# Eight-expert transformer tower on one core: the middle stage's steps in another order, and h1 carried inside the routed rows

## Chip, cores and metric

The kernel is one program on 1 core of one Trainium2 chip. The metric is the device time of one execution in microseconds. Before the change it is 1646.1 us (median of 3 runs, 1643.71 to 1647.52).

## What is computed

x holds 16 images of 256x256. The reference runs five parts on them; every LayerNorm here is over the last axis.

```python
h = tok(x)                                   # three Haar levels, gated, and put together again
h = _layernorm(h + attention(h))             # 16 heads; this is h1 in the kernel
h = _layernorm(h + ffn0(h))                  # h2: top 2 of 8 experts, 256 -> 512 -> 256
h = _layernorm(h + L1_attn(h))               # h3, see below
h = _layernorm(h + ffn1(h))                  # top 1 of 8 experts, 256 -> 1024 -> 256

# ffn0
gates, expert_idx = jax.lax.top_k(probs, K)  # K = 2
out = jnp.einsum('ne,nec->nc', weights, expert_out)

# L1_attn
attn_out = quantum_circuit(xh)               # cumprod(cos(v)) over groups of 16
x1 = layer_norm(x + attn_out, gamma1, beta1)
q = quantum_circuit(x1[..., :nq])            # nq = 16
h = jnp.einsum('btq,fq->btf', q, w1) + b1
ffn_out = jnp.einsum('btf,cf->btc', jax.nn.relu(h), w2) + b2
return layer_norm(x1 + ffn_out, gamma2, beta2)
```

## The kernel before

The program has four stages, one behind the other, with a barrier (the semaphores quiet0, quiet1, quiet2) between them.

**Attention** makes h1 image by image (16 images of 256 tokens, two tiles of 128 partitions each). Its step `nrm` writes h1 to a tile of rows of 264 words: 256 of h1, two expert numbers, two gates, two target rows, and two words that are zero. `rows` scatters each row twice to `rows0_d`, one copy per chosen expert. `store` (L387 to L389, SyncE) writes h1 itself to `h1_d` in HBM, and `nrm` waits for it two images later (L1008).

**First experts** (`experts`) takes 71 tiles of 128 routed rows. Per tile GpSimd gathers the rows (L1123), TensorE transposes, multiplies, transposes and multiplies (L1155, L1164, L1186, L1176), and VectorE adds the first bias (L1256). `owner` (L1237 to L1249) then finds for each row which of its two choices this expert is, its gate and its target row. `g2` adds the second bias (L1263) and multiplies by the gate (L1266). GpSimd sends the result to `y0_d` (L1128), whose first 4096 rows are the first choices and whose next 4096 are the second.

**Middle** (`middle`) takes 16 images again. The order on all engines comes from one list, STEPS. Each engine walks through it once per turn and runs those steps that it has a function for, with an image number that the second word gives as an offset to the turn:

```python
STEPS = [("load", "n2"), ("A1", "n"), ("root0", "n"), ("h2", "n"), ("SC", "m"), ("root1", "m"), ("RTa", "n"), ("x1", "m"),
         ("T", "p"), ("XQ", "m"), ("qsin", "m"), ("D", "p"), ("rk", "p"), ("RTb", "n"), ("sin", "n"), ("prep", "n"),
         ("SQa", "m"), ("qc", "m"), ("x1g", "m"), ("R2", "f"), ("root2", "f"), ("SQb", "m"), ("F1", "m"), ("R", "p"), ("scatter", "p"),
         ("B2", "f"), ("A0", "n1"), ("root3", "f"), ("h2b", "n"), ("F2", "m"), ("h3", "f")]
AHEAD = {"n2": 2, "n1": 1, "n": 0, "m": -1, "f": -2, "p": -3}
```

So in a full turn four images are under way. The steps, by what they do:

- A0 (GpSimd, L1415): h1 + first choice. A1 (VectorE, L1689): that + second choice, then its mean and variance (variances 0: L1671, L1674, and the negated mean, L1681).
- root0 to root3 (GpSimd, L1419 to L1424): 1/sqrt of a variance and the offset. h2 (ScalarE, L1557): the normalized h2; its second half (L1570, L1572) counts the whole turns in the cosine's argument. h2b (GpSimd, L1438): h2 + beta2.
- RTa, RTb (VectorE, L1695, L1702): the argument less whole turns. sin (ScalarE, L1594 to L1597): the cosines. SC (VectorE, L1709, L1711): the running products by a scan, + h2, variances 1. x1 (ScalarE, L1557): the normalized x1. x1g (GpSimd, L1431): x1 * gamma1.
- XQ, qsin, SQa, qc, SQb (L1720 to L1727, L1606 to L1609, L1734, L1616 and L1617, L1739): the same circuit on 16 columns of x1.
- F1 (TensorE L1483 and L1490, ScalarE L1623 and L1628): transposes, first product and Relu. F2 (TensorE L1499 to L1506): second product. R2, B2 (VectorE): variances 2, then z2 and r3 (L1753, L1762) and variances 3. h3 (ScalarE): the normalized h3.
- T (TensorE L1516 and L1524, ScalarE L1634): h3 transposed and the logits. D (VectorE L1773 to L1783): the choice. rk (TensorE), R (VectorE L1788 to L1794): ranks. scatter (GpSimd L1444, L1447): two indirect DMAs of h3's rows.
- prep (all engines, for image 0 only): the weights transposed; on SyncE it prefetches the next stage's weights.

Numbers of images count from 0; "turn" below means one pass through STEPS, and a full turn is one in which all four images exist (13 of them, with A1 of images 3 to 15).

**Last experts** takes 39 tiles of h3 and is not touched.

## Time and profile before

| | us |
|---|---|
| median of 3 runs | 1646.1 |
| profiled execution | 1646.75 |
| its span, first to last instruction | 1644.9 |
| TensorE busy | 1301.9 (79%) |
| VectorE busy | 930.9 (57%) |
| GpSimd busy | 733.7 (45%) |
| ScalarE busy | 526.1 (32%) |

The page writes PE for TensorE, PEld for its weight loads, DVE for VectorE, ACT for ScalarE, POOL for GpSimd and SP for SyncE (SPq is its queue, where DMAs are issued). Busy time is an average over the four stages, which have different limits; so the windows and the timelines of single stages matter more than these shares. In a timeline a row gives the start, the duration, the engine, the line, the operation with output and input, and in brackets how long the engine sat idle before and what ended that. Attention ends at about 613 us, first experts at 917, middle at 1305.

### The profile page before, as it was taken

To read this page: it belongs to the slowest core of one execution; us is meant where nothing else is said; L and a number is where in the kernel's file an instruction comes from. 1 tells how busy PE (TensorE), PEld (TensorE's weight loads), DVE (VectorE), ACT (ScalarE), POOL (GpSimd) and SP (SyncE) were. 2 spreads that over 40 slices of the span, in tenths; PEclk is the share of its full clock that TensorE was granted. 3 is DMA by queue.
4 is the path that set the end of the run, shared out by engine and by line. 5 is a ranking of instruction groups with operands and counts; after the bars stand their busy time and mean duration, and the time that the engine had idled before them with its cause. 6 is when DMAs were issued, how large, how long until landed. Compare 5 with 4: busy or idle time off the path is not lost.

```text
span 1644.9 us, 23467 instructions
## 1 busy us (share of the span) xinstructions
PE 1301.9 (79%) x6856; PEld 913.8 (56%) x6856; DVE 930.9 (57%) x2664; ACT 526.1 (32%) x998; POOL 733.7 (45%) x926
## 2 busy tenths in 40 slices
...
DMA packets 97448, 134.69 MB, mean 82 GB/s; under 512 B 18208, under 2 KB 80302, under 8 KB 96304
## 3 DMA queue, kind: packets, MB, share of 16 engines
...
q10 hardware_dynamic: 3376, 1.22, 0.4%
q8 instruction: 61, 1.00, 0.3%
...
## 4 chain that ended last, share of the span: by engine, by line
PE 57%; DVE 16%; POOL 9%; issue 6%; ACT 5%; DMA 4%; SPq 1%; another core or an unknown queue 1%; ACTq 0%; DVEq 0%; POOLq 0%
PE ebank L1942 8%; PE ebank L1953 8%; PE ebank L1164 8%; PE ebank L1176 7%; PE mbank L1506 4%; PE bank L597 3%; DVE top_a_a L967 2%; PE ebank L1963 2%; PE ebank L1186 2%; PE bank L679 2%; PE av_bank L653 2%; POOL fine_a L454 1%; PE s_bank L620 1%; DVE product_a L852 1%; DMA prob_a<-in_L_attn_Wo 1%
## 5 line engine op out<-in xcount | busy, mean ns | idle before, releaser
L967 DVE TENSOR_REDUCE top_a_a<-s_bank 128x4 f32<-128x1024 f32 x128 | 156.5, 1223 | 122.6 <-PE s_bank L620 113.2
L796 ACT ACTIVATE prob_a<-s_bank 128x1024 f32<-128x1024 f32 x128 | 130.4, 1019 | 80.7 <-PE s_bank L641 76.9
L1942 PE MATMUL ebank<-w,exT 128*128 x312 | 143.0, 602 | 0.7 <-ACT exT L1988 0.7
L1506 PE MATMUL mbank<-w2T_m,fhT_m 128*128 128x256 f32 x512 | 143.0, 443 | 0.0
L1953 PE MATMUL ebank<-w,ehT 128*128 x624 | 141.2, 379 | 0.9 <-ACT ehT L1996 0.9
L1164 PE MATMUL ebank<-w,exT 128*128 x284 | 135.4, 600 | 0.6 <-ACT exT L1211 0.6
L1176 PE MATMUL ebank<-w,ehT 128*128 x568 | 134.4, 380 | 0.8 <-ACT ehT L1217 0.8
L1506 PEld LDWEIGHTS mbank<-w2T_m,fhT_m 128*128 128x128 f32 x512 | 119.0, 232 | 23.1
L1123 POOL DMA_INDIRECT ex<-rows_d,tile_row x71 | 72.8, 1025 | 119.6 <-DVE sent_to L1249 103.6
L1953 PEld LDWEIGHTS ebank<-w,ehT 128*128 128x128 f32 x624 | 115.6, 190 | 15.7 <-issue 1.6
L531 POOL DMA_INDIRECT rows_d<-h_a,row_i_a x64 | 63.7, 995 | 128.8 <-DVE row_i_a L1053 113.8
L1176 PEld LDWEIGHTS ebank<-w,ehT 128*128 128x128 f32 x568 | 102.5, 190 | 12.5 <-issue 1.5
L1256 DVE TENSOR_TENSOR eh<-ebank,b 128x512 f32<-128x512 f32 x71 | 49.1, 692 | 104.9 <-PE ebank L1164 103.5
L2027 DVE TENSOR_TENSOR eh<-ebank,b 128x512 f32<-128x512 f32 x78 | 54.0, 692 | 84.9 <-PE ebank L1942 84.9
L620 PE MATMUL s_bank<-ks_a,qs_a 48*128 48x256 f32 x512 | 67.6, 344 | 31.7 <-DVE top_a_a L967 19.2
L1128 POOL DMA_INDIRECT y_d<-ey,sent_to x71 | 72.2, 1017 | 42.4 <-issue 27.9
L1942 PEld LDWEIGHTS ebank<-w,exT 128*128 128x128 f32 x312 | 57.2, 193 | 58.7 <-issue 58.7
L1996 ACT ACTIVATE ehT<-ebank 128x512 f32<-128x512 f32 x78 | 42.3, 595 | 138.7 <-PE ebank L1963 138.7
L1419 POOL TENSOR_SCALAR rstd_m_m<-moments_m_m 128x2 f32<-128x2 f32 x64 | 34.2, 535 | 115.8 <-DVE moments_m_m L1674 88.9
L1217 ACT ACTIVATE ehT<-ebank 128x512 f32<-128x512 f32 x71 | 42.4, 597 | 131.6 <-PE ebank L1186 129.7
L620 PEld LDWEIGHTS s_bank<-ks_a,qs_a 48*128 48x128 f32 x512 | 42.0, 202 | 72.4 <-issue 48.2
L641 PE MATMUL s_bank<-qs_a,ks_a 50*128 50x256 f32 x512 | 66.5, 340 | 17.2 <-DMA qs_a<-shiftT_a 13.9
...
## 6 DMA issues: line engine op xcount, KB each, us to landing
...
```

Of the source, the lines that this page charges most:

```text
L531: pool.indirect_dma_start(out=rows0_d, out_offset=bass.IndirectOffsetOnAxis(ap=row_i[i % 2][:, t, k:k + 1], axis=0), in_=h1[i % 2][:, t, : ...
L620: last = nc.tensor.matmul(s1_bank[:, g, t * SEQ:(t + 1) * SEQ], qs[i % RING][rows, j, t * P:(t + 1) * P], ks[i % RING][rows, j, :], start= ...
L641: last = nc.tensor.matmul(s2_bank[:, g, t * SEQ:(t + 1) * SEQ], ks[i % RING][rows, j, t * P:(t + 1) * P], qs[i % RING][rows, j, :], start= ...
L796: nc.scalar.activation(prob[:, j % 4].rearrange("p g t s -> p (g t s)"), s2_bank[:].rearrange("p g s -> p (g s)"), ACT.Exp, scale=HD ** -0 ...
L967: nc.vector.tensor_reduce(top[:, j].rearrange("p g t -> p (g t)"), s1_bank[:].rearrange("p g (t s) -> p (g t) s", t=TPI), axis=AX, op=ALU. ...
L1123: pool.indirect_dma_start(out=x[j % XR][:].bitcast(I32), out_offset=None, in_=rows_d, bounds_check=E * SLOTS - 1, oob_is_err=False, in_off ...
L1128: pool.indirect_dma_start(out=y_d, out_offset=bass.IndirectOffsetOnAxis(ap=sent_to[j % YR][:], axis=0), in_=y[j % YR][:], in_offset=None, ...
L1164: last = nc.tensor.matmul(bank[1 + j % 2][:], xT[j % 2][:, ch, :], w[:, bass.ds(e, 1), width * ch:width * (ch + 1)].rearrange("p a f -> p ...
L1176: last = nc.tensor.matmul(bank[4 + j % 2][:, 0:D], hT[j % 2][:, f, :], w[:, bass.ds(e, 1), at:at + D].rearrange("p a d -> p (a d)"), start ...
L1506: last = nc.tensor.matmul(b[:, t * D:(t + 1) * D], hT[:, f, t * P:(t + 1) * P], w2T[:, f, :], start=False, stop=f == FC - 1)
L1942: last = nc.tensor.matmul(bank[1 + n % 2][:], xT[j % 2][:, ch, :], w[:, bass.ds(e, 1), at:at + 512].rearrange("p a f -> p (a f)"), start=c ...
L1953: last = nc.tensor.matmul(bank[4 + j % 2][:, 0:D], hT[j % 2][:, f, :], w[:, bass.ds(e, 1), at:at + D].rearrange("p a d -> p (a d)"), start ...
```

## The change

Two things change.

1. **h1 travels with the rows.** The two spare words of each row now hold 1.0 for the first choice and 0.0 for the second. `owner` picks that word together with the gate and the target row, and writes h1 times it (h1 or nothing) to the result tile y. `g2` adds the second bias into a tile of its own, and then computes gate * result + y in one operation. So `y0_d`'s first half holds h1 + first choice. `h1_d`, its stores in attention, its loads in middle, the semaphores for both and step A0 are gone; A1 adds the two halves.
2. **STEPS in another order**, with h2's second half as a step of its own (tn), and F1's transposes as a step of their own (qT). The offsets stay.

```diff
--- attention
-                 ("p2_6", "t"), ("av_2", "t"), ("p1_6", "n"), ("tprd_4", "n2"), ("lg", "p"), ("store", "p"),
+                 ("p2_6", "t"), ("av_2", "t"), ("p1_6", "n"), ("tprd_4", "n2"), ("lg", "p"),
...
-            def store(i):
-                sp.wait_ge(q["h1_ok"], i + 1)
-                sp.dma_start(h1_v[i], h1[i % 2][:, :, 0:D]).then_inc(h1_out[i % 2], 16)
...
-                c.run(nc.gpsimd.memset(h1[u][:, :, D:ROW0], 0.0))
+                c.run(nc.gpsimd.memset(h1[u][:, :, D + 6:D + 7], 1.0))
+                c.run(nc.gpsimd.memset(h1[u][:, :, D + 7:D + 8], 0.0))
...
-                    dve.wait_ge(h1_out[i % 2], 16 * (i // 2))
--- experts
                 c.link(nc.vector.scalar_tensor_tensor(
-                    out=chosen[:], in0=tail[:, D:D + 2].unsqueeze(1).to_broadcast([P, 2, 2]), scalar=tile_sum[:, j:j + 1],
-                    in1=tail[:, D + 2:D + 6].rearrange("p (a k) -> p a k", k=2), op0=ALU.is_equal, op1=ALU.mult))
+                    out=chosen[:], in0=tail[:, D:D + 2].unsqueeze(1).to_broadcast([P, 3, 2]), scalar=tile_sum[:, j:j + 1],
+                    in1=tail[:, D + 2:D + 8].rearrange("p (a k) -> p a k", k=2), op0=ALU.is_equal, op1=ALU.mult))
                 c.link(nc.vector.tensor_reduce(own[u][:], chosen[:], axis=AX, op=ALU.add))
-                nc.vector.tensor_tensor(sent_to[u][:], own[u][:, 1:2], outside[:, j:j + 1], ALU.max).then_inc(own_ok, 1)
+                c.run(nc.vector.tensor_tensor(sent_to[u][:], own[u][:, 1:2], outside[:, j:j + 1], ALU.max))
+                nc.vector.tensor_scalar(y[u][:], tail[:, 0:D], own[u][:, 2:3], None, ALU.mult).then_inc(own_ok, 1)
...
-                nc.vector.tensor_tensor(y[u][:], bank[4 + j % 2][:, 0:D], b[:, bass.ds(e, 1), width:width + D].rearrange("p a f -> p (a f)"),
+                if j >= 1:
+                    dve.wait_ge(y_ok, j)
+                nc.vector.tensor_tensor(result[:], bank[4 + j % 2][:, 0:D], b[:, bass.ds(e, 1), width:width + D].rearrange("p a f -> p (a f)"),
                                         ALU.add).then_inc(biased, 1)
                 dve.wait_ge(biased, j + 1)
-                nc.vector.tensor_scalar(y[u][:], y[u][:], own[u][:, 0:1], None, ALU.mult).then_inc(y_ok, 1)
+                dve.wait_ge(own_ok, j + 1)
+                nc.vector.scalar_tensor_tensor(out=y[u][:], in0=result[:], scalar=own[u][:, 0:1], in1=y[u][:], op0=ALU.mult, op1=ALU.add).then_inc(y_ok, 1)
--- middle
-        STEPS = [("load", "n2"), ("A1", "n"), ("root0", "n"), ("h2", "n"), ("SC", "m"), ("root1", "m"), ("RTa", "n"), ("x1", "m"),
...
+        STEPS = [("load", "n2"), ("A1", "n"), ("root0", "n"), ("SC", "m"), ("h2", "n"), ("root1", "m"), ("x1", "m"), ("h2b", "n"), ("tn", "n"),
+                 ("XQ", "m"), ("qsin", "m"), ("T", "p"), ("RTa", "n"), ("RTb", "n"), ("prep", "n"), ("SQa", "m"), ("R2", "f"), ("x1g", "m"),
+                 ("qc", "m"), ("SQb", "m"), ("sin", "n"), ("root2", "f"), ("D", "p"), ("qT", "m"), ("rk", "p"), ("B2", "f"), ("root3", "f"),
+                 ("R", "p"), ("F1", "m"), ("h3", "f"), ("scatter", "p"), ("F2", "m")]
...
             constants()
-            for i in range(RING):
-                load_h(i)
             sp.wait_ge(s["quiet1"], 4)
-            load_y(0)
-            load_y(1)
+            load(0)
+            load(1)
             more_constants()
-            load_y(2)
+            load(2)
...
-            def A0(i):
-                u = i % RING
-                pool.wait_ge(h_in[u], 32 * (i // RING + 1))
-                nc.gpsimd.tensor_tensor(hin[u][:], hin[u][:], ya[u][:], ALU.add).then_inc(q["part_ok"], 1)
...
-                dve.wait_ge(q["part_ok"], i + 1)
-                dve.wait_ge(y_in[u], 16 * (i // RING + 1))
+                dve.wait_ge(y_in[u], 32 * (i // RING + 1))
...
-                nc.vector.tensor_tensor(flat(sum_), flat(hin[u]), flat(yb[u]), ALU.add).then_inc(q["sum_ok"], 1)
+                nc.vector.tensor_tensor(flat(sum_), flat(ya[u]), flat(yb[u]), ALU.add).then_inc(q["sum_ok"], 1)
```

How the new list moves instructions, at three places.

GpSimd in middle, from one image's scatter to the next image's root0, before. In these rows moments and off belong to root3, then root0, and h_0, h_1 are tiles of h3 (from token) or h2 (for h2b):

```order
L1444 COPY h_0_m<-token_m 128x2x4
L1447 DMA rows_d<-h_0_m,row_i_m 33792x260 x2
L1415 TENSOR_TENSOR hin_m<-hin_m,ya_m 128x512
L1419 TENSOR_SCALAR rstd_m_m<-moments_m_m 128x2
L1423 TENSOR_TENSOR rstd_m_m<-rstd_m_m,minus_half 128x2
L1424 TENSOR_TENSOR off_m_m<-minus_m_m,rstd_m_m 128x2
L1438 TENSOR_TENSOR h2b_m<-h_1_m,a_be_m 128x512
L1419 TENSOR_SCALAR rstd_m_m<-moments_m_m 128x2
L1423 TENSOR_TENSOR rstd_m_m<-rstd_m_m,minus_half 128x2
L1424 TENSOR_TENSOR off_m_m<-minus_m_m,rstd_m_m 128x2
```

and with the change, from root3 on, where root3, scatter, root0, root1 and h2b follow one another:

```order
L1403 TENSOR_SCALAR rstd_m_m<-moments_m_m 128x2
L1407 TENSOR_TENSOR rstd_m_m<-rstd_m_m,minus_half 128x2
L1408 TENSOR_TENSOR off_m_m<-minus_m_m,rstd_m_m 128x2
L1428 COPY h_0_m<-token_m 128x2x4
L1431 DMA rows_d<-h_0_m,row_i_m 33792x260 x2
L1403 TENSOR_SCALAR rstd_m_m<-moments_m_m 128x2
L1407 TENSOR_TENSOR rstd_m_m<-rstd_m_m,minus_half 128x2
L1408 TENSOR_TENSOR off_m_m<-minus_m_m,rstd_m_m 128x2
L1403 TENSOR_SCALAR rstd_m_m<-moments_m_m 128x2
L1407 TENSOR_TENSOR rstd_m_m<-rstd_m_m,minus_half 128x2
L1408 TENSOR_TENSOR off_m_m<-minus_m_m,rstd_m_m 128x2
L1422 TENSOR_TENSOR h2b_m<-h_0_m,a_be_m 128x512
```

A0 (L1415) is gone, the scatter stands behind root3 and directly ahead of root0, and h2b behind root1.

ScalarE in middle, from h3 to x1, before:

```order
L1557 ACTIVATE h_1_m<-r_m,off_m_m,rstd_m_m 128x256 x2
L1557 ACTIVATE h_0_m<-sum__m,off_m_m,rstd_m_m 128x256 x2
L1570 ACTIVATE turnsn_m<-h_0_m,magic_m 128x512
L1572 ACTIVATE turnsn_m<-turnsn_m,off_magic_m 128x512
L1557 ACTIVATE x__m<-sum_m,off_m_m,rstd_m_m 128x256 x2
```

and with the change:

```order
L1543 ACTIVATE h_1_m<-r_m,off_m_m,rstd_m_m 128x256 x2
L1543 ACTIVATE h_0_m<-sum__m,off_m_m,rstd_m_m 128x256 x2
L1543 ACTIVATE x__m<-sum_m,off_m_m,rstd_m_m 128x256 x2
L1558 ACTIVATE turnsn_m<-h_0_m,magic_m 128x512
L1560 ACTIVATE turnsn_m<-turnsn_m,off_magic_m 128x512
```

x1 now stands directly behind h2, and the two turns operations behind it.

VectorE in middle, the middle part of a turn, before (q_arg is XQ, lg to both is D, arg is RTb, q_run is SQa, the statistics of mbank are R2, qstack is SQb):

```order
L1727 TENSOR_SCALAR q_arg_m<-q_arg_m 128x32
L1773 COPY lg_m<-mbank 128x16
L1776 MAX best_m<-lg_m 128x8 x2
L1779 MAX_INDEX where_m<-best_m,lg_m 128x8 x2
L1780 TENSOR_TENSOR away_59<-lg_m,best_m 128x16
L1782 CAST idx_f_m<-where_m 128x2
L1783 TENSOR_TENSOR both_m<-iota_52,idx_f_m 128x16
L1702 SCALAR_TENSOR_TENSOR arg_m<-turnsn_m,rest_m 128x512
L1734 SCALAR_TENSOR_TENSOR q_run_m<-q_cos_m,q_first_m 128x32
L1671 BN_STATS stats_m_m<-mbank 128x6 x2
L1674 BN_AGGR moments_m_m<-stats_m_m 128x2 x2
L1739 TENSOR_TENSOR qstack_m<-q_run_m,qstack_m 128x2x16
```

and with the change (rest is RTa):

```order
L1716 TENSOR_SCALAR q_arg_m<-q_arg_m 128x32
L1684 SCALAR_TENSOR_TENSOR rest_m<-turnsn_m,h_1_m 128x512
L1691 SCALAR_TENSOR_TENSOR arg_m<-turnsn_m,rest_m 128x512
L1723 SCALAR_TENSOR_TENSOR q_run_m<-q_cos_m,q_first_m 128x32
L1661 BN_STATS stats_m_m<-mbank 128x6 x2
L1664 BN_AGGR moments_m_m<-stats_m_m 128x2 x2
L1728 TENSOR_TENSOR qstack_m<-q_run_m,qstack_m 128x2x16
L1762 COPY lg_m<-mbank 128x16
L1765 MAX best_m<-lg_m 128x8 x2
```

RTa has come in behind XQ, and D stands behind SQb.

## Rows read from the trace of the kernel before

**Rows 1.** Windows by stage: length; PE, PEld, DVE, ACT, POOL busy; clock, DMA, GB/s.

```profile
622.00:912.00 290.00, 288.48 (x1267) 199.75 (x1266) 135.27 (x424) 69.20 (x141) 139.00 (x137) 1.00 0.18 58
...
925.00:1215.00 290.00, 200.91 (x804) 156.29 (x805) 215.35 (x668) 139.10 (x294) 154.17 (x215) 0.72 0.27 88
```

**Rows 2.** Timeline, VectorE, one turn of middle: start, duration (us), operation, [idle before].

```profile
1080.30 0.88 DVE L1762 SCALAR_TENSOR_TENSOR r_m<-z_m,rstd_m_m,h2b_m 128x256 f32<-128x256 f32 x2
...
1082.35 1.31 DVE L1681 TENSOR_SCALAR minus_m_m<-moments_m_m 128x2 f32<-128x2 f32 x1
...
1083.66 0.69 DVE L1689 TENSOR_TENSOR sum__m<-hin_m,yb_m 128x512 f32<-128x512 f32 x1
...
1085.54 2.30 DVE L1709 TENSOR_TENSOR_SCAN prods_m<-cosv_m,cos_first_m 128x512 f32<-128x512 f32 x1
...
1089.67 0.17 DVE L1681 TENSOR_SCALAR minus_m_m<-moments_m_m 128x2 f32<-128x2 f32 x1
...
1092.15 0.69 DVE L1695 SCALAR_TENSOR_TENSOR rest_m<-turnsn_m,h_m 128x512 f32<-128x512 f32 x1 [2.31 <-ACT turnsn_m L1572]
...
1093.14 0.19 DVE L1720 TENSOR_TENSOR xq_m<-x__m,a_g_m 128x32 f32<-128x32 f32 x1 [0.29 <-ACT x__m L1557]
...
1099.58 0.19 DVE L1739 TENSOR_TENSOR qstack_m<-q_run_m,qstack_m 128x32 fp32r<-128x32 f32 x1 [0.83 <-ACT qstack_m L1617]
```

**Rows 3.** Timeline of GpSimd, the same turn.

```profile
1079.94 1.11 POOL L1447 DMA_INDIRECT rows_d<-h_m,row_i_m  x1 [1.32 <-DVE row_i_m L1794]
...
1082.35 1.28 POOL L1415 TENSOR_TENSOR hin_m<-hin_m,ya_m 128x512 f32<-128x512 f32 x1
...
1085.47 1.29 POOL L1438 TENSOR_TENSOR h2b_m<-h_m,a_be_m 128x512 f32<-128x512 f32 x1
...
1091.02 0.19 POOL L1424 TENSOR_TENSOR off_m_m<-minus_m_m,rstd_m_m 128x2 f32<-128x2 f32 x1
```

**Rows 4.** Timeline of ScalarE, the same turn.

```profile
1092.03 1.08 ACT L1557 ACTIVATE x__m<-sum_m,off_m_m,rstd_m_m 128x256 f32<-128x256 f32 x2
```

**Rows 5.** Timeline, VectorE then GpSimd, third turn of middle (no third norm yet).

```profile
956.92 1.23 DVE L1709 TENSOR_TENSOR_SCAN prods_m<-cosv_m,cos_first_m 128x512 f32<-128x512 f32 x1
...
959.51 0.20 POOL L1424 TENSOR_TENSOR off_m_m<-minus_m_m,rstd_m_m 128x2 f32<-128x2 f32 x1
```

**Rows 6.** Timeline of SyncE, VectorE and ScalarE at the start of middle.

```profile
919.16 2.58 SPq L1364 DMA_DIRECT2D hin_m<-h_d  x3
...
929.14 0.69 DVE L1689 TENSOR_TENSOR sum__m<-hin_m,yb_m 128x512 f32<-128x512 f32 x1 [9.71 <-POOL hin_m L1415]
...
942.49 1.71 ACT L1552 ACTIVATE w2T_m<-mbank 128x512 f32<-128x512 f32 x3 [0.26 <-PE mbank L1471]
```

**Rows 7.** Timeline of VectorE, third and fourth turn of middle.

```profile
969.92 0.76 DVE L1671 BATCH_NORM_STATS2 stats_m_m<-mbank 128x6 f32<-128x256 f32 x2 [2.73 <-PE mbank L1506]
...
975.27 0.69 DVE L1689 TENSOR_TENSOR sum__m<-hin_m,yb_m 128x512 f32<-128x512 f32 x1
```

**Rows 8.** Timeline of VectorE, then TensorE, in the last turns of middle.

```profile
1255.49 1.22 DVE L1709 TENSOR_TENSOR_SCAN prods_m<-cosv_m,cos_first_m 128x512 f32<-128x512 f32 x1
...
1292.78 0.88 DVE L1753 SCALAR_TENSOR_TENSOR z_m<-mbank,moments_m_m,a_g_m 128x256 f32<-128x256 f32 x2 [0.90 <-POOL rstd_m_m L1421]
...
1304.81 0.16 DVE L1794 SCALAR_TENSOR_TENSOR row_i_m<-idx_f_m,rank 128x2 int32<-128x2 f32 x1
...
1272.42 1.23 PE L1490 MATMUL mbank<-qT_m,wq_m 80*128 80x256 f32 x4 [0.47 <-ACT qT_m L1623]
...
1286.47 0.60 PE L1516 MATMUL mbank<-ident,h_m 128*128 128x128 f32 x4
```

**Rows 9.** Timeline of VectorE, then GpSimd, in one tile of first experts.

```profile
754.68 0.42 DVE L1263 TENSOR_TENSOR ey<-ebank,b 128x256 f32<-128x256 f32 x1 [0.68 <-PE ebank L1176]
...
755.14 0.35 DVE L1266 TENSOR_SCALAR ey<-ey,own 128x256 f32<-128x256 f32 x1
...
754.84 1.03 POOL L1123 DMA_INDIRECT ex<-rows_d,tile_row  x1 [1.62 <-DVE sent_to L1249]
```

More of the change, by code:

```diff
@@ L118, in tower @@
     with ctx:
-        h0_d, h1_d = (dram(n, (TOKENS, D)) for n in ("h0_d", "h1_d"))
+        h0_d = dram("h0_d", (TOKENS, D))
         rows0_d = dram("rows0_d", (E * SLOTS, ROW0), I32)
@@ L165, in tower @@
         with nc.Block() as block:
-            used = attention(nc, block, a, s, zones("_a"), ctx0, load_weights, h0_d, h1_d, rows0_d, ident, before, ones, iota8, cnt,
+            used = attention(nc, block, a, s, zones("_a"), ctx0, load_weights, h0_d, rows0_d, ident, before, ones, iota8, cnt,
                              lane, tile_no, ones8, sends0, minus_half)
@@ L169, in tower @@
             ctx0.close()
-            middle(nc, block, a, s, ctx, zones("_m"), load_weights, lambda sp, e: load_bias(sp, 1, bias1, e, s["w_in1"][e]), h1_d, y0_d, rows1_d, ident, before, ones, iota8, cnt, away1, rank1, minus_half)
+            middle(nc, block, a, s, ctx, zones("_m"), load_weights, lambda sp, e: load_bias(sp, 1, bias1, e, s["w_in1"][e]), y0_d, rows1_d, ident, before, ones, iota8, cnt, away1, rank1, minus_half)
             last_experts(nc, block, s, ctx, zone1, weights1, bias1, load_weights, load_bias, rows1_d, gate1_d, out, cnt, rank1, away1,
@@ L211, in tile_maps, with attention @@
     return build, tile_sum, tile_expert, row_i, outside
-def attention(nc, block, a, s, zone, sems, load_weights, h0_d, h1_d, rows0_d, ident, before, ones, iota8, cnt, lane, tile_no, ones8, sends0,
+def attention(nc, block, a, s, zone, sems, load_weights, h0_d, rows0_d, ident, before, ones, iota8, cnt, lane, tile_no, ones8, sends0,
               minus_half):
@@ L298, in attention @@
         q = {n: sem("a_" + n) for n in names}
-        x_in, h1_out, shift_in = (sem.pair("a_" + n) for n in ("x_in", "h1_out", "shift_in"))
+        x_in, shift_in = (sem.pair("a_" + n) for n in ("x_in", "shift_in"))
         rows_out = [s["rows_out0"], s["rows_out0_odd"]]
@@ L1079, in experts @@
     y = [sb(f"ey{u}", [P, D]) for u in range(YR)]
-    chosen = sb("chosen", [P, 2, 2])
-    own = [sb(f"own{u}", [P, 2]) for u in range(YR)]
+    chosen = sb("chosen", [P, 3, 2])
+    own = [sb(f"own{u}", [P, 3]) for u in range(YR)]
+    result = sb("result", [P, D])
     sent_to = [sb(f"sent_to{u}", [P, 1], I32) for u in range(YR)]
@@ L1273, in _, with middle @@
                     g2(j - 1)
-            dve.wait_ge(own_ok, count)
+            dve.wait_ge(c.sem, c.n)
             c.reset()
             nc.vector.drain().then_inc(s["quiet1"], 1)
-def middle(nc, block, a, s, ctx, zone, load_weights, load_bias, h1_d, y0_d, rows1_d, ident, before, ones, iota8, cnt,
+def middle(nc, block, a, s, ctx, zone, load_weights, load_bias, y0_d, rows1_d, ident, before, ones, iota8, cnt,
            away1, rank1, minus_half):
     sem = Semaphores(nc, ctx)
-    h1_v = h1_d.rearrange("(i t p) d -> i p t d", t=TPI, p=P)
     y_v = y0_d.rearrange("(k i t p) d -> k i p t d", k=2, t=TPI, p=P)
@@ L1299, in middle @@
         w2T = sb("w2T", [P, FC, D])
-        hin = [sb(f"hin{u}", [P, TPI, D]) for u in range(RING)]
         ya, yb = ([sb(f"{n}{u}", [P, TPI, D]) for u in range(RING)] for n in ("ya", "yb"))
@@ L1384, in prefetch, with later @@
                     load_bias(sp, i // 2 - 5)
-            def load(i):
+            def later(i):
                 if i >= RING:
-                    load_h(i)
-                    load_y(i)
+                    load(i)
             constants()
-            for i in range(RING):
-                load_h(i)
             sp.wait_ge(s["quiet1"], 4)
-            load_y(0)
-            load_y(1)
+            load(0)
+            load(1)
             more_constants()
-            load_y(2)
-            turns({"load": load, "prep": prefetch})
+            load(2)
+            turns({"load": later, "prep": prefetch})
             sp.sem_inc(s["quiet2"], 1)
```

29 lines of the change are left out of this document (13 added, 16 removed), and 3 rows, old and new, of the table STEPS.

## Prediction

> **What bounds the kernel now.** I read four views, in this order. The windows by stage say which engine is full. First experts has TensorE busy for 288.48 of 290 us and VectorE for 135.27; middle has TensorE at 200.91, VectorE at 215.35, POOL at 154.17, and nobody full [rows 1]. So first experts is held by TensorE, and middle by a chain that goes round all engines. The change leaves TensorE's work alone in both, so its gain must come from middle, and the question in first experts is only whether its new VectorE work stays hidden. The timelines of one turn of middle then show the chain's links, and those of the first and last turns show what a full turn doesn't.
>
> In middle VectorE runs through its list, and three kinds of time are not work. (1) The scan L1709 takes 2.30 us in a full turn and 1.23 in the third turn [rows 2, 5]. In the full turn it starts at 1085.54, and POOL's h2b, a 128x512 addition, runs from 1085.47 for 1.29 [rows 3]. The scan waits until that is over. (2) The negation L1681 of 2 elements takes 1.31 at 1082.35 and 0.17 at 1089.67 [rows 2]; at 1082.35 POOL starts A0's addition, 1.28 long [rows 3]. (3) VectorE is idle for 2.31 us before L1695, 0.29 before L1720 and 0.83 before L1739, each time on ScalarE [rows 2]: from var1 (1089.67 + 0.17 = 1089.84) to x1's first use at 1093.14 are 3.30 us. POOL had finished root1 at 1091.21 (1091.02 + 0.19) [rows 3], but ScalarE began x1 only at 1092.03 [rows 4], since h2 and the two turns operations stand ahead of it. A turn lasts 21.55 us on the mean: 13 of them from 975.27 to 1255.49, 280.2 us [rows 7, 8].
>
> **The change in a full turn of middle.** I lay VectorE's new list out with these durations, from A1's start.
> - h2b stands behind root1 on POOL, at a time when VectorE waits for x1 anyway: the scan goes back from 2.30 to 1.23, **-1.07**.
> - A0 is gone, so the negation goes from 1.31 to 0.17, **-1.14**. A1 adds two tiles, as before, and costs the same.
> - qc stands ahead of sin on ScalarE, and R2 ahead of SQb on VectorE: the 0.83 before L1739 goes, **-0.83**.
> - x1 comes directly behind h2. h2 needs root0, whose last step ended at 959.71 in the third turn, 2.79 after the scan's start at 956.92 [rows 5]. VectorE's var1 comes 3.22 after that start (4.30 from 1085.54 to 1089.84, less 1.07), and root1 1.37 later (1089.84 to 1091.21), so h2 (two ScalarE instructions, about the 1.08 of x1's) is over before root1 is. Then x1 starts 0.12 after root1 and takes 1.08: from var1 to the first use 1.37 + 0.12 + 1.08 + 0.03 = 2.60 for 3.30, **-0.70**.
> - RTa, which filled that gap, now stands behind XQ, in line: 0.69 and a wait of 0.03, **+0.72**. RTb, SQa, R2, SQb, D, B2 and R keep their durations and only change places, **0**.
> - D follows SQb and needs the logits. ScalarE's copy for them stands behind qsin, and TensorE's eight matmuls behind that; laid out they end 0.1 after VectorE is ready, **+0.10**.
> - scatter moves behind root3 on POOL's queue, ahead of the next root0. POOL takes up root3 when B2's negation is done, 0.97 before the next A1; root3 needs about 1.6 with the block by A1's addition, and the scatter's copy and two indirect DMAs (L1447, 1.11 for one [rows 3]) about 3.0. That leaves POOL free some 4.0 us into the next turn, where root0 could start at 2.0 but would be blocked by the scan until 3.1: root0 ends about 0.6 later than in rows 5, root1 follows it at once, and x1's first use slips by **+0.17**. From here on POOL's queue is as long as VectorE's, and each further microsecond on it counts.
>
> Sum: -2.75 us per full turn, 13 times: **-35.8**. What hides the rest: TensorE needs 14.05 us from F1's first matmul to the next T (1272.42 to 1286.47 [rows 8]); F1 starts 14.6 us into the new turn of 18.8, so T comes at about 9.9 of the next, and D's copy needs it by 11.3.
>
> **The first turns.** SyncE no longer issues the three h1 loads, 2.58 us, ahead of the first y loads [rows 6], and 0.75 MB less stand before them in the queues. A0's addition (1.28) goes from the first path, but the second of two loads must now be waited for, issued 0.5 later. I take **-2.8** for A1's first start (now 929.14 [rows 6]); bounds -1.3, if the second load eats the rest, and -4.
> Against this, prep now precedes sin on ScalarE. Its six copies end at 944.20 (942.49 + 1.71 [rows 6]); image 0's sine and its table load, some 2.9 us so far run beside VectorE's preparation, come behind them, and the first scan waits for them. Laid out, the first x1 comes 5 us later, but the third turn's R2 waited 2.73 for TensorE at 969.92 [rows 7] and part is absorbed: F1(0) starts 3.0 later, and R2(0) and the fourth turn with it, **+3.0**.
>
> **The last turns.** From the scan of 1255.49 to R's end at 1304.97 (1304.81 + 0.16) are 49.5 us [rows 8]. Here TensorE's 14.05 of F1 and F2 are on the path. F1(15) starts 16.93 after that scan (1272.42) and would start at 13.9: the negation blocked by h2b, the copy of T ahead of qsin and R ahead of F1 no longer stand before it, **-3.0**. In the turn behind, D and R stand ahead of B2(15), which starts 6.31 after T (1286.47 to 1292.78 [rows 8]). In the new list R2 and root2 run while D waits for its logits, and R follows B2: 3.6, **-2.7**. Together -5.7.
>
> **First experts.** Per tile the new tensor_scalar of a row tile costs what L1266 does, 0.35, and the closing scalar_tensor_tensor with two SBUF inputs 0.44 (0.88 for two [rows 2]) for 0.35. VectorE is idle 0.68 before L1263 [rows 9] and far more before the next tile: **0** per tile, +0.1 at the end. own_ok comes 0.4 later, so POOL's load too; it has three tiles, 12 us, before TensorE wants it, 0. Floor: these cannot gain. **Attention.** 16 stores of 256 KB and their waits leave SyncE, the next load starts earlier; nothing on the chain of waits names them: 0, bounds 0 and -4.
>
> Total: -35.8 - 2.8 + 3.0 - 5.7 + 0.1 = -41.2. The profiled execution took 1646.75 (span 1644.9), so 1605.5; the median of the runs, 1646.1, is 0.65 lower, so **1605**.
>
> **A rule weighed.** The indirect DMA of 1.11 us at 1079.94 ran beside L1762 at 1080.30, which reads two SBUF tiles for 0.88 [rows 2, 3], and it was not held for as long as that. In the new order the scatter's second DMA lies beside the scan and the addition behind it, of the same kind. The Trainium skill (SBUF — State Buffer, Who interferes with whom) says that VectorE and GpSimd share one port pair, that the one that starts second waits for the whole instruction, and that an indirect DMA from GpSimd is kept from writing its descriptors by VectorE operations in a two-port mode. The first half agrees with the 2.30 and the 1.31 above. The second half would speak against this change if it held for scans and additions too, which the page leaves to inference for additions: that is the first rival. The sum without it is 1605, with it 1630.
>
> **The rivals.**
> - POOL's queue sets the turn. Mechanism: the second indirect DMA is held for the scan (1.23) and the addition (0.69), so root0, h2, root1 and x1 all come 1.9 later: 13 x 1.9 = +25, **1630**. For: POOL now has no slack. Against: the 1.11 beside two-input work.
> - First experts turns slower, past the gain. Place: POOL's loop of load and send, which starts at own_ok. A tile takes 4.1 us (290 us for 71 [rows 1]), and POOL is idle 1.62 of it before L1123 [rows 9]; I count half of that as slack, since the rest passes between own_ok and the load's start. If the new 0.35 and 0.44 on VectorE each hold a descriptor write, the slack is used up; beyond that point every 0.1 us costs 71 x 0.1 = 7 us, and 0.7 us more gives +50, **1655**. Against: L1266 at 755.14 lies beside the load at 754.84, which takes 1.03 all the same [rows 9].
> - The order doesn't do what it says: x1 gains nothing, because h2 waits on root0 behind scatter, and the early turns cost double. Then only the two port blocks go, 13 x (-1.07 - 1.14 + 0.3) = -25, **1621**.
> - More than forecast: SyncE's shorter queue also speeds attention by its bound of 4 us, and the logits and scatter terms (0.27 x 13 = 3.5) vanish: **1597**.
>
> **How the numbers follow.** Forecast 0.58 (own range 1599 to 1613, from the bounds of the start and half a microsecond per turn). 1621 has 0.15, 1630 has 0.12, 1597 and below 0.10, the slower case 0.05. The range 1594 to 1631 leaves out the slower case, the far half of 1597 and of 1630. A measurement of this kernel can tell about 0.2% (3.3 us) from no change. All cases but one lie lower by far more: faster 0.94, same 0.01, slower 0.05.
>
> **What would show it.** A1 to A1 at 18.8 us in full turns; the scan at 1.23; the negation at 0.17; no idle before SQb; x1's first use 2.8 after var1; GpSimd never idle from root3 to root1; the first scan of middle late. First experts must stay at 4.1 us per tile. Turns of 20.5 or more with an indirect DMA over 2 us would prove the first rival; a TensorE with idle time in first experts the second.

## The result, and the profile after

The changed kernel takes 1596.56 us (median of 4 runs, 1594.2 to 1599.27) against 1645.63 before: ratio 0.9702, 95% interval 0.9683 to 0.9722. The profiled execution took 1596.87 us, its span is 1595.1, 49.8 less than before. The forecast was 1605, with a range of 1594 to 1631 (1599 to 1613 for the forecast's own case).

The same windows by stage as in [rows 1]: length; PE, PEld, DVE, ACT, POOL busy; clock, DMA share, GB/s.

```profile
622.00:912.00 290.00, 289.17 (x1270) 200.54 (x1268) 162.67 (x492) 68.92 (x140) 139.99 (x137) 1.00 0.18 58
925.00:1215.00 290.00, 227.88 (x934) 179.01 (x935) 216.87 (x771) 157.06 (x339) 139.36 (x231) 0.75 0.23 73
```

First experts has 27 us more VectorE work in 290 us and a TensorE that is as full as before. In middle VectorE is as busy as before (216.87 against 215.35), but does more in it: 771 instructions for 668. The time came out of held and waiting instructions.

A full turn on VectorE, against [rows 2]: start, duration, operation, [idle before].

```profile
1085.20 0.69 DVE L1678 TENSOR_TENSOR sum__m<-ya_m,yb_m 128x512 f32<-128x512 f32 x1
...
1087.08 1.23 DVE L1698 TENSOR_TENSOR_SCAN prods_m<-cosv_m,cos_first_m 128x512 f32<-128x512 f32 x1
...
1090.14 0.17 DVE L1671 TENSOR_SCALAR minus_m_m<-moments_m_m 128x2 f32<-128x2 f32 x1
1092.90 0.19 DVE L1709 TENSOR_TENSOR xq_m<-x__m,a_g_m 128x32 f32<-128x32 f32 x1 [2.59 <-ACT x__m L1543]
1093.13 1.15 DVE L1710 TENSOR_TENSOR xq_m<-xq_m,a_be_m 128x32 f32<-128x32 f32 x1
...
1097.91 0.16 DVE L1728 TENSOR_TENSOR qstack_m<-q_run_m,qstack_m 128x32 fp32r<-128x32 f32 x1
1098.03 0.17 DVE L1762 COPY lg_m<-mbank 128x16 f32<-128x16 f32 x1
...
1102.45 0.17 DVE L1671 TENSOR_SCALAR minus_m_m<-moments_m_m 128x2 f32<-128x2 f32 x1
...
1103.47 0.69 DVE L1678 TENSOR_TENSOR sum__m<-ya_m,yb_m 128x512 f32<-128x512 f32 x1
```

The turn is 18.27 us, the scan 1.23 (2.30 before), the negation ahead of the next A1 0.17 (1.31), SQb and D wait for nothing (D only just: by the trace its logits end 0.03 before its copy begins), and XQ starts 2.76 after var1's negation (3.47). One held instruction is left: L1710, a 32-column addition, takes 1.15 us.

GpSimd in the same turn, against [rows 3].

```profile
1086.37 1.12 POOL L1431 DMA_INDIRECT rows_d<-h_m,row_i_m  x1 [0.29 <-POOL h_m L1428]
1087.80 1.27 POOL L1431 DMA_INDIRECT rows_d<-h_m,row_i_m  x1 [0.31 <-issue]
1089.09 0.25 POOL L1403 TENSOR_SCALAR rstd_m_m<-moments_m_m 128x2 f32<-128x2 f32 x1
...
1091.48 0.20 POOL L1408 TENSOR_TENSOR off_m_m<-minus_m_m,rstd_m_m 128x2 f32<-128x2 f32 x1
1091.71 1.26 POOL L1422 TENSOR_TENSOR h2b_m<-h_m,a_be_m 128x512 f32<-128x512 f32 x1
1092.94 1.28 POOL L1415 TENSOR_TENSOR x1g_m<-x__m,a_g_m 128x512 f32<-128x512 f32 x1
```

Its queue is closed from root3 to x1g, and x1g stands beside XQ: it is what holds L1710. The second indirect DMA, from 1087.80 to 1089.07, lies beside the last 0.51 us of the scan and the whole addition behind it (0.69 from 1088.34). It takes 1.27 us, where the second one of a pair took 0.97 before, so the two held it for 0.3 us at most and not for their own length.

ScalarE, against [rows 4]: x1 comes 0.09 after root1's end at 1091.68.

```profile
1091.77 1.09 ACT L1543 ACTIVATE x__m<-sum_m,off_m_m,rstd_m_m 128x256 f32<-128x256 f32 x2
```

The first turns on VectorE, against [rows 6, 7], and the last ones, against [rows 8] (T is TensorE's).

```profile
925.64 0.69 DVE L1678 TENSOR_TENSOR sum__m<-ya_m,yb_m 128x512 f32<-128x512 f32 x1 [7.23 <-DMA yb_m<-y_d]
...
943.68 1.23 DVE L1698 TENSOR_TENSOR_SCAN prods_m<-cosv_m,cos_first_m 128x512 f32<-128x512 f32 x1 [6.41 <-ACT cos_first_m L1585]
...
969.77 0.76 DVE L1661 BATCH_NORM_STATS2 stats_m_m<-mbank 128x6 f32<-128x256 f32 x2 [3.82 <-PE mbank L1492]
...
975.09 0.69 DVE L1678 TENSOR_TENSOR sum__m<-ya_m,yb_m 128x512 f32<-128x512 f32 x1
...
1213.39 1.22 DVE L1698 TENSOR_TENSOR_SCAN prods_m<-cosv_m,cos_first_m 128x512 f32<-128x512 f32 x1
...
1243.65 0.88 DVE L1742 SCALAR_TENSOR_TENSOR z_m<-mbank,moments_m_m,a_g_m 128x256 f32<-128x256 f32 x2
...
1255.75 0.16 DVE L1783 SCALAR_TENSOR_TENSOR row_i_m<-idx_f_m,rank 128x2 int32<-128x2 f32 x1
```

```profile
1226.84 1.20 PE L1476 MATMUL mbank<-qT_m,wq_m 80*128 80x256 f32 x4
...
1239.92 0.60 PE L1502 MATMUL mbank<-ident,h_m 128*128 128x128 f32 x4
```

First experts, VectorE in one tile, against [rows 9]: the row times 1 or 0, and the closing operation.

```profile
756.88 0.35 DVE L1244 TENSOR_SCALAR ey<-ex,own 128x256 f32<-128x256 f32 x1
757.63 0.42 DVE L1260 TENSOR_TENSOR result<-ebank,b 128x256 f32<-128x256 f32 x1 [0.40 <-PE ebank L1170]
758.09 0.48 DVE L1264 SCALAR_TENSOR_TENSOR ey<-result,own,ey 128x256 f32<-128x256 f32 x1
```

Where the 49.8 us went, stage by stage, from the starts of A1 and the rows above:

| stretch | before | after | change | forecast |
|---|---|---|---|---|
| to first experts' first matmul | 617.14 | 615.64 | -1.5 | 0 |
| from there to A1(0): first experts and middle's start | 312.0 | 310.0 | -2.0 | -2.7 |
| A1(0) to A1(3): first turns | 46.13 | 49.45 | +3.3 | +3.0 |
| A1(3) to the last scan: the 13 full turns | 280.2 | 238.3 | -41.9 | -35.8 |
| last scan to R's end | 49.5 | 42.5 | -7.0 | -5.7 |
| last experts | 339.9 | 339.2 | -0.7 | 0 |

Kernels below that share the changed kernel's attention reach that first matmul between 610.2 and 620.9 us. The first row's 1.5 us is therefore no finding.

### The profile page after: what moved, and what is told of

Its sections match the earlier page's. It is cut to its first block, busy times and chain, and to the rows that moved or that the text cites. A ratio compares the mean times of both kernels' runs of the same rounds, so it can differ in the third digit from the quotient of the medians.

```text
span 1595.1 us, 23616 instructions
## 1 busy us (share of the span) xinstructions
PE 1306.6 (82%) x6856; PEld 916.3 (57%) x6856; DVE 927.7 (58%) x2735; ACT 523.6 (33%) x998; POOL 697.3 (44%) x912
## 3 DMA queue, kind: packets, MB, share of 16 engines
q10 hardware_dynamic: 3376, 1.22, 0.4%
## 4 chain that ended last, share of the span: by engine, by line
PE 58%; DVE 16%; POOL 11%; issue 6%; DMA 4%; ACT 3%; SPq 2%; ACTq 0%; DVEq 0%; POOLq 0%
PE ebank L1931 9%; PE ebank L1942 8%; PE ebank L1158 8%; PE ebank L1170 8%; PE bank L591 3%; DVE top_a_a L961 2%; PE av_bank L647 2%; PE mbank L1492 2%; PE ebank L1952 2%; PE ebank L1180 2%; PE bank L673 2%; POOL rows_d L1431 2%; PE s_bank L614 2%; POOL rstd_m_m L1407 2%; PE s_bank L635 2%
## 5 line engine op out<-in xcount | busy, mean ns | idle before, releaser
L1403 POOL TENSOR_SCALAR rstd_m_m<-moments_m_m 128x2 f32<-128x2 f32 x64 | 16.3, 255 | 159.5 <-DVE minus_m_m L1671 90.5
L647 PE MATMUL av_bank<-prob_a,vx_a 128*32 128x256 f32 x1024 | 82.9, 450 | 1.1 <-ACT prob_a L790 1.1
```

What stands on the lines that cost most here:

```text
L647: last = nc.tensor.matmul(av_bank[32 * j:32 * j + 32, 0:SEQ], vx[i % RING][:, t, head(k, j), :], prob[:, (2 * k + j % 2) % 4, j // 2, t, : ...
```

## The experiments

Twelve kernels ran, each compared with the kernel before on the same chip. On those chips the kernel before took 1644.4 to 1651.8 us (medians), so a time expected in microseconds is compared with the ratio times 1646, and a difference "against the changed kernel" is that of the two ratios times 1646. "Turn" is from A1 to A1; "12 turns" is from A1(3) to A1(15): 259.35 us before, 220.04 after.

**1. h2b alone moved, in the kernel before.**

```diff
-... ("SC", "m"), ("root1", "m"), ("RTa", "n"), ... ("A0", "n1"), ("root3", "f"), ("h2b", "n"), ("F2", "m"), ...
+... ("SC", "m"), ("root1", "m"), ("h2b", "n"), ("RTa", "n"), ... ("A0", "n1"), ("root3", "f"), ("F2", "m"), ...
```

> The kernel before, with h2b alone moved from behind root3 to behind root1 in STEPS. Block theory: the scan no longer waits for h2b's addition on GpSimd (2.30 to 1.23 us), x1 follows it, a full turn is 1.07 shorter, 13 turns give -14: about 1632 us. Rival (the chain runs over root0, h2 and the turns operations, and the longer scan only fills VectorE's idle time): no change, 1646.

Measured: ratio 0.9926, interval 0.9909 to 0.9943 (-12 us). The 12 turns took 246.75, 1.05 less each. VectorE in one turn:

```profile
1079.03 1.32 DVE L1681 TENSOR_SCALAR minus_m_m<-moments_m_m 128x2 f32<-128x2 f32 x1
...
1082.22 1.23 DVE L1709 TENSOR_TENSOR_SCAN prods_m<-cosv_m,cos_first_m 128x512 f32<-128x512 f32 x1
```

The scan is free and the negation still held, beside A0. The scan's 1.07 is this block and nothing else. But the usual turn is 20.49 for 21.36, only 0.87 less: D's copy starts 0.27 after the start of XQ's last operation, for 0.09 before, and by the trace 0.03 after the end of the logits, so some 0.18 go into a wait for them. The mean gains more because the odd turns of about 22 us are gone. The first turns lost 2.1 us of it (A1(0) to A1(3) 48.26 for 46.13).

**2. h1's part alone: the changed kernel with the old list.**

```diff
-        STEPS = [("load", "n2"), ("A1", "n"), ("root0", "n"), ("SC", "m"), ("h2", "n"), ...
+        STEPS = [("load", "n2"), ("A1", "n"), ("root0", "n"), ("h2", "n"), ("tn", "n"), ("SC", "m"), ("root1", "m"), ("RTa", "n"), ...
```

> The changed kernel with the old order (A0, store and h1's loads gone, result computed in first experts). Block theory: only the negation behind B2 gets shorter (1.31 to 0.17) since A0 is gone, the scan stays at 2.30: 13 x -1.14 = -15, the start -2.5, attention -1.0, drain about -0.5: about 1627 us. Rival (the removal of A0 and the transfers is nearly all of the gain): 1605 or less. Second rival (first experts pay for it): its tiles over 4.15 us, above 1635.

Measured: 0.9889, 0.9872 to 0.9907 (-18 us). The mirror image of run 1:

```profile
1082.37 0.17 DVE L1671 TENSOR_SCALAR minus_m_m<-moments_m_m 128x2 f32<-128x2 f32 x1
...
1084.32 2.30 DVE L1698 TENSOR_TENSOR_SCAN prods_m<-cosv_m,cos_first_m 128x512 f32<-128x512 f32 x1
```

Here too the usual turn comes down to 20.49, 0.87 less, and D waits 0.23 to 0.26 for its logits in it. From the first matmul of first experts to A1(0) it needs 309.4 us for 312.0, as the changed kernel does (310.0). The earlier start and the free negation thus belong to h1's part.

**3. The order alone: the kernel before with the new list, A0 behind root2.**

```diff
-... ("sin", "n"), ("root2", "f"), ("D", "p"), ...
+... ("sin", "n"), ("root2", "f"), ("A0", "n1"), ("D", "p"), ...
```

(against the changed kernel's list; h1 is stored, loaded and added as before).

> The kernel before (h1 stored, loaded and added by A0) with the new order, A0 put behind root2. Order theory: full turns of 18.3 to 18.7 us, since A0 meets GpSimd idle and VectorE on operations with one SBUF input: 13 x -3.1, drain -7, first turns +3.3: about 1602 us (1600 to 1608). Rival: A0 blocks small VectorE operations one after the other, +1.2 per turn: 1617.

Measured: 0.9789, 0.9772 to 0.9806 (-35 us, or 1611): above the theory's 1600 to 1608 and below the rival's 1617. The mechanism is close to the rival's, but one small operation is held per turn and not one after the other. The usual turn is 19.14, 0.88 above the changed kernel's. GpSimd's A0, and VectorE beside it, first in a usual turn:

```profile
1090.60 1.26 POOL L1415 TENSOR_TENSOR hin_m<-hin_m,ya_m 128x512 f32<-128x512 f32 x1
```

```profile
1090.53 0.17 DVE L1788 CAST idx_f_m<-where_m 128x2 f32<-128x2 uint32 x1
1090.73 1.16 DVE L1789 TENSOR_TENSOR both_m<-iota,idx_f_m 128x16 bf16<-128x16 f32 x1
1091.81 0.86 DVE L1759 SCALAR_TENSOR_TENSOR z_m<-mbank,moments_m_m,a_g_m 128x256 f32<-128x256 f32 x2
```

and then in one of the four turns of 19.44 to 19.49:

```profile
1109.73 1.26 POOL L1415 TENSOR_TENSOR hin_m<-hin_m,ya_m 128x512 f32<-128x512 f32 x1
```

```profile
1109.80 1.21 DVE L1788 CAST idx_f_m<-where_m 128x2 f32<-128x2 uint32 x1
1111.05 0.17 DVE L1789 TENSOR_TENSOR both_m<-iota,idx_f_m 128x16 bf16<-128x16 f32 x1
```

I had put A0 there because D's operations are small and most have one SBUF input. Size doesn't matter: L1789 (0.17 by itself) waited until A0 was over at 1091.86. Nor is one input enough: the cast of 2 elements took 1.21 (0.17 by itself) where it began after A0, which was so in those four turns. The index searches ended before A0 or within 0.11 us of its start, so no run says whether they would be held. Removing A0 was worth as much under the new order (0.88 per turn) as under the old (run 2: 0.87 in the usual turn, 12 turns in 248.49, 0.91 each).

**4. A pad on GpSimd ahead of root0, changed kernel.** The pad is a memset of 128x512.

```diff
+            def pad_(i):
+                c.link(nc.gpsimd.memset(pad[:], 0.0))
-... ("scatter", "p"), ("F2", "m")]
+... ("scatter", "p"), ("F2", "m"), ("pad", "n")]
```

> The changed kernel with one memset of 128x512 (about 0.55 us with its wait) on GpSimd between scatter and the next root0, once per turn. If GpSimd's queue from root3 to root1 has no slack, x1 slips by as much: 13 to 16 turns x 0.55 = +7 to +9, about 1605 us. If VectorE's list alone sets the turn and root0 has slack: 1597, no change.

Measured: 0.9755, 0.9738 to 0.9772; usual turn 18.83, 0.57 longer, for a pad of

```profile
1057.75 0.55 POOL L1436 MEMSET pad_m<- 128x512 f32 x1
```

XQ's wait for x1 grew from 2.59 to 3.16. GpSimd's queue has no slack between root3 and root1, as the prediction said.

**5. The same pad behind x1g**, meant as a control.

```diff
-... ("x1g", "m"), ("qc", "m"), ...
+... ("x1g", "m"), ("pad", "n"), ("qc", "m"), ...
```

> Control of the pad before root0: the same memset behind x1g, where GpSimd is idle for 3.9 us. Every theory: no change, 1597 us (within 2).

Measured: 0.9738, 0.9718 to 0.9757; usual turn 18.51, 0.25 longer, where I expected nothing. GpSimd, then VectorE:

```profile
1093.86 0.52 POOL L1436 MEMSET pad_m<- 128x512 f32 x1
```

```profile
1093.99 0.42 DVE L1715 TENSOR_SCALAR q_turns_m<-xq_m 128x32 f32<-128x32 f32 x1
```

L1715 (0.18 by itself) was held by the pad. GpSimd had 3.86 us to spare there and the pad still cost half of its own length. A place that is free on GpSimd's queue is not free if VectorE works beside it.

**6. prep behind sin, changed kernel.**

```diff
-... ("RTb", "n"), ("prep", "n"), ("SQa", "m"), ... ("sin", "n"), ("root2", "f"), ...
+... ("RTb", "n"), ("SQa", "m"), ... ("sin", "n"), ("prep", "n"), ("root2", "f"), ...
```

> The changed kernel with prep moved behind sin in STEPS, so that image 0's cosines come before the six copies on ScalarE. If the late first scan costs the +3.3 us of the first three turns: -3, about 1593.5 us, and A1 of image 3 starts 3 us earlier. Rival (the first F2 sets that time anyway, whatever precedes it): 1596.5.

Measured: 0.9667, 0.9651 to 0.9683 (-5.8 us against the changed kernel), twice what I expected. VectorE, first scan, R2 of the third turn and the fourth A1:

```profile
924.93 0.69 DVE L1678 TENSOR_TENSOR sum__m<-ya_m,yb_m 128x512 f32<-128x512 f32 x1 [6.48 <-DMA yb_m<-y_d]
...
937.41 1.22 DVE L1698 TENSOR_TENSOR_SCAN prods_m<-cosv_m,cos_first_m 128x512 f32<-128x512 f32 x1
...
963.21 0.76 DVE L1661 BATCH_NORM_STATS2 stats_m_m<-mbank 128x6 f32<-128x256 f32 x2 [3.50 <-PE mbank L1492]
...
968.53 0.69 DVE L1678 TENSOR_TENSOR sum__m<-ya_m,yb_m 128x512 f32<-128x512 f32 x1
```

The wait of 6.41 before the first scan is gone and A1(0) to A1(3) takes 43.60 for 49.45, the usual turn staying at 18.25. R2's wait for TensorE is 3.50 here and 3.82 with prep early, so it absorbed nothing.

**7. R and scatter one turn later, changed kernel** (a new offset "o" of -4; R behind root1, scatter behind x1g).

```diff
-... ("root1", "m"), ("x1", "m"), ... ("x1g", "m"), ("qc", "m"), ... ("root3", "f"), ("R", "p"), ("F1", "m"), ("h3", "f"), ("scatter", "p"), ("F2", "m")]
+... ("root1", "m"), ("R", "o"), ("x1", "m"), ... ("x1g", "m"), ("scatter", "o"), ("qc", "m"), ... ("root3", "f"), ("F1", "m"), ("h3", "f"), ("F2", "m")]
```

> The changed kernel with R and scatter taken one turn later, R in VectorE's 2.59 us gap behind var1, scatter behind x1g. VectorE's list gets 0.93 shorter per turn; if VectorE's list sets the turn: 17.4 us per turn, 13 x -0.93 = -12, about 1585 us. If TensorE's F1, F2 and T come too late for D then: half of it, -5 to -6, 1591. If GpSimd's queue alone set the turn (root3, scatter, root0, root1), the scatter's 3 us off it would give more than 0.93 per turn: below 1584.

Measured: 0.9657, 0.9641 to 0.9672 (-7.4 us, or 1589.5: between the two first cases; the third is out). R goes into VectorE's wait for x1, but the usual turn is 17.53, 0.73 less and not 0.93. x1g now begins just before XQ (at 1065.54) and holds its first operation instead of its second, whose 0.19 then comes behind:

```profile
1065.66 1.20 DVE L1709 TENSOR_TENSOR xq_m<-x__m,a_g_m 128x32 f32<-128x32 f32 x1 [2.00 <-ACT x__m L1543]
```

And two of the 12 turns take 18.44 and 18.27. In the first of these TensorE and VectorE read:

```profile
1059.07 6.07 PE L1492 MATMUL mbank<-w2T_m,fhT_m 128*128 128x256 f32 x16
```

```profile
1071.76 0.17 DVE L1762 COPY lg_m<-mbank 128x16 f32<-128x16 f32 x1 [0.69 <-PE mbank L1510]
```

In the turn before, the same 16 matmuls took 4.61. The granted clock over them was 0.59 of the upper level, 2.4 GHz, and 0.78 in the turn before: more of them ran at the lower level, 1.2 GHz (the 16 of the second half, at a clock of 1.00, take 3.62). T came late, and D waited for its logits. The four turns of about 22 us in the kernel before show the same: D waits 0.49 to 0.84 for the logits there.

**8. Image 0's y loads ahead of the constants, changed kernel.**

```diff
-            constants()
             sp.wait_ge(s["quiet1"], 4)
             load(0)
-            load(1)
+            constants()
             more_constants()
+            load(1)
```

> The changed kernel with the first y loads issued ahead of the constants (w2n is 1 MB) on SyncE. If the first A1 waits for its tile behind w2n: it starts 2.5 us earlier, -2.5, about 1594 us. Rival (prep then waits for the constants, which land later): 1596.5 or slower.

Measured: 0.9692, 0.9677 to 0.9707 (-1.6 us, within its interval of nothing). A1(0) came 305.3 us after the first matmul of first experts in place of 310.0, but A1(0) to A1(3) took 52.44 for 49.45, because prep's constants now come later: its cast at 931.20 waits 1.22 us for a DMA, and the first scan comes 20.7 us after A1(0), for 18.0. Most of the gain is given back.

**9. Runs 6 and 7 together.**

> The changed kernel with both edits that gained alone: prep behind sin, and R and scatter one turn later. Theory: they act in different places (first turns; every full turn), so their gains add: 0.9667 and 0.9657 against the changed kernel's 0.9702 give 0.9702 - 0.0035 - 0.0045 = 0.9622 (about 1583 us against a kernel before of 1645). In the trace the gap from the second image's A1 to the third's goes to 12.3 us, as with prep late alone, and the full turns are 17.5. Rival: both gains come from the same early turns (R's delay also takes POOL work out of them), and the ratio stays at 0.9655.

Measured: 0.9630, 0.9608 to 0.9652, for 0.9622 expected. A1(0) to A1(3) is 43.66 and the 12 turns 212.13, each as in the run alone (43.60; 212.18): the gains add.

**10. x1g waits until SQa has ended, changed kernel.**

```diff
                 pool.wait_ge(q["x1_ok"], i + 1)
+                pool.wait_ge(q["qrun_ok"], i + 1)
```

> The changed kernel, but GpSimd's x1g waits until SQa has ended, so that it runs beside R2's statistics, which VectorE reads from PSUM, and no longer beside XQ. Theory: GpSimd's 128x512 additions and products hold VectorE's next SBUF operation until they end. In the changed kernel XQ's L1710 takes 1.20 us for that, 0.19 by itself; so 0.95 us go, and SQb (behind R2's 0.98) is now held for at most 0.5: -0.4 to -0.9 per turn, 15 turns, ratio 0.962 to 0.967. The logits for D are copied behind qsin and move with XQ, so D does not wait. Rival 1: GpSimd has no slack there (root2 comes late, B2 waits) and the turn stays at 18.3: ratio 0.970. Rival 2: the statistics from PSUM are held as well, R2 takes 2 us in place of 0.73, ratio 0.970 to 0.972.

Measured: 0.9675, 0.9652 to 0.9699 (-4.4 us), just outside the range expected, and its interval overlaps the changed kernel's; the 12 turns, 215.34 for 220.04, carry the argument. GpSimd, then VectorE:

```profile
1078.69 1.26 POOL L1416 TENSOR_TENSOR x1g_m<-x__m,a_g_m 128x512 f32<-128x512 f32 x1 [3.35 <-DVE q_run_m L1724]
```

```profile
1075.49 0.19 DVE L1711 TENSOR_TENSOR xq_m<-xq_m,a_be_m 128x32 f32<-128x32 f32 x1
...
1078.38 0.74 DVE L1662 BATCH_NORM_STATS2 stats_m_m<-mbank 128x6 f32<-128x256 f32 x2
1079.15 0.25 DVE L1665 BATCH_NORM_AGGREGATE moments_m_m<-stats_m_m 128x2 f32<-128x6 f32 x2
1079.65 0.34 DVE L1729 TENSOR_TENSOR qstack_m<-q_run_m,qstack_m 128x32 fp32r<-128x32 f32 x1 [0.26 <-ACT qstack_m L1606]
1080.53 0.17 DVE L1763 COPY lg_m<-mbank 128x16 f32<-128x16 f32 x1 [0.54 <-PE mbank L1511]
```

The addition is back at 0.19, the statistics, which read PSUM, stay at 0.74 with x1g beginning in their middle (0.76 at 1221.86, where they began 0.82 after it), and their aggregation at 0.25 beside it. The usual turn is 17.77 (-0.49), inside the -0.4 to -0.9 expected; but about every fourth is 18.4, since D now waits for the logits, which I had excluded.

**11. Control: x1g waits until XQ has ended** (`q["xq_ok"]` in place of `q["qrun_ok"]`).

> Control for the run before: x1g waits until XQ has ended, so that it runs beside RTa and RTb, which read SBUF. Theory: L1710 goes back to 0.19, but RTa or RTb is held by as much; turn 18.1 to 18.6, ratio 0.968 to 0.975. Rival (only the place in XQ, ahead of ScalarE's small circuit, costs): turn 17.5, ratio 0.962.

Measured: 0.9702, 0.9679 to 0.9724, turn 18.19. XQ is free and RTb is held instead (0.69 by itself):

```profile
1079.38 1.63 DVE L1692 SCALAR_TENSOR_TENSOR arg_m<-turnsn_m,rest_m 128x512 f32<-128x512 f32 x1
```

So the gain of run 10 comes from what VectorE does beside x1g, not from XQ being early.

**12. All: runs 6, 7 and 10, with scatter ahead of x1g.**

> All together: prep late, R and scatter late, scatter ahead of x1g on GpSimd, and x1g behind SQa. Theory: with R late the loop over TensorE (F1, F2, T, logits, D, rk, F1) already sets the turn (D's copy waited 0.69 for the logits at a turn of 17.5), so the 0.95 us that XQ wins back goes into a longer wait before D: turn 17.3 to 17.5, ratio 0.960 to 0.962, hardly below the run without x1g's move. Rival: TensorE has slack, and the turn goes to 16.9: ratio 0.956.

Measured: 0.9589, 0.9571 to 0.9608, median 1582.45 (1576.18 to 1584.22) against 1651.8 for the kernel before on that chip: the fastest version here, below both kernels. It is 0.004 below run 9, with intervals that touch, and lies between the theory (0.960 to 0.962) and its rival (0.956). In the trace, which is of the fastest execution, the 12 turns take 206.88, 17.24 each, and fall from 17.64 to 17.09; in a late one:

```profile
1084.30 0.70 DVE L1729 TENSOR_TENSOR qstack_m<-q_run_m,qstack_m 128x32 fp32r<-128x32 f32 x1
1084.93 0.17 DVE L1763 COPY lg_m<-mbank 128x16 f32<-128x16 f32 x1
```

So the loop over TensorE does not hold the turn at 17.5, as the theory had it. It is not idle either: in the first eight full turns, 17.64 down to 17.10, D's copy begins 0.03 to 0.04 after the end of the logits, though the profile names no wait. Only at 17.09 does the gap grow (0.06 to 0.08), and there VectorE's list sets the turn, with the wait for x1 and one hold of half a microsecond. The two are nearly level, so freeing that hold was not shown to gain more.

## Why the prediction was right

The forecast mechanism is what happened, and the time came 8.4 us below it: inside the range, but below the 1599 to 1613 of the forecast's own case. By the table, 6.1 us of that lie in the full turns and 1.3 in the last ones. Term by term, in a full turn:

- **Scan -1.07**: 2.30 to 1.23. Alone, in run 1, it gave 0.87 in the usual turn (1.05 on the mean), since D then waited for its logits. Right in the new order, where no such wait shows.
- **Negation -1.14**: 1.31 to 0.17. Alone, in run 2, it gave 0.87 for the same reason, and run 3 returns 0.88 when A0 comes back in another place. Right.
- **SQb's wait -0.83**: gone, and from R2 to SQb 0.92 less. Right.
- **x1 earlier -0.70**: negation to XQ 3.47 to 2.76, -0.71. Right.
- **RTa in line +0.72**: right (RTa and RTb together take 1.32 up to SQa, where RTb alone took 0.60).
- **D waits +0.10**: absent. In the regular turn the logits come as VectorE is ready, 0.03 to 0.05 before D's copy.
- **Scatter delays x1 +0.17**: absent. root0 ended 3.34 after the scan's start, the 3.39 laid out, but root1's turn came just then: at 1090.39, 0.08 after var1's negation had ended (1090.14 + 0.17). The error is in the step "root1 follows it at once, and x1's first use slips": there was exactly as much room as root0 needed. Run 4 shows that not 0.55 more would fit.
- **Not foreseen**: the mean of 21.55 held four turns of 21.96 to 22.36 (21.36 otherwise) in which D waited 0.49 to 0.84 for the logits. They are nearly gone (18.26 usual, 18.33 on the mean), some 0.1 us per turn: 0.19 between mean and usual turn before, 0.07 now. I took the mean as the base and subtracted terms of a regular turn.

Together -3.2 for -2.75 per turn, or -41.9 for -35.8.

**First turns +3.0**, measured +3.3: a right number from two wrong halves. Run 6 shows that prep ahead of sin costs 5.85, not 3.0, since R2's wait absorbs none of it; with prep late the first turns take 43.6 for 46.13, so the new order saves 2.5 there, which I hadn't counted. The step that failed is "part is absorbed". **Start -2.8**: measured -2.5 from the last tile's end, from h1's part by run 2. **Last turns -5.7**, measured -7.0: F1(15) 13.45 after the scan for 16.93 (-3.5 for -3.0), B2(15) 3.73 after T for 6.31 (-2.6 for -2.7), and -1.0 because F1 to T took 13.08 for 14.05, which I held fixed; the granted clock over that stretch was 0.76 for 0.71. **First experts +0.1**: +0.5 by the last tile's end, no loss per tile; the closing operation took 0.48 for 0.44.

The rivals: the first (1630) needed an indirect DMA held for the scan and the addition, 1.9 us; beside the last 0.51 us of the scan and the whole addition it took 1.27, some 0.3 more than before. The Trainium skill (SBUF — State Buffer, Who interferes with whom) leaves to inference that an addition with two SBUF inputs doesn't starve the descriptor writing; the trace agrees, with that delay of 0.3 at most. For a scan the runs show less: in no run did such a DMA lie beside more than 0.52 us of one. The second (1655) fell with a TensorE busy for 289.17 of 290 us. The third (1621) is excluded by the turn of 18.26. Of the fourth (1597) the part with the logits and the scatter came true, 3.5 us; its 4 us in attention did not show (1.5, inside the spread between runs). The odd turns and the last turns, which it doesn't name, made up the rest, so that its number fits is luck.

One assumption was only half right: that h2b costs nothing "when VectorE waits for x1 anyway". h2b itself holds little (L1709 took 0.31 in one turn and 0.19 in the 15 others). But x1g behind it holds L1710 for about 1 us in every turn, before and after, which I overlooked in the kernel before: there the same line took 1.14. It was the next thing to gain, and run 12 gains half of it.

What stays open: why TensorE's lower level falls on another part of F2 in single turns was not tried.
